# A gated attention and feed-forward block on one core: the mask as one row, fp16 row maxima, constant products in TensorE's early waits, and the range check's squares moved to turns 3 to 6

## The reference

```
logits = einsum('bhqd,bhkd->bhqk', Q * 32**-0.5, K) + b        # Q from layernorm(x), 8 heads of 32
weights = softmax(logits - 1e30 * (1 - mask))                  # mask is 1 only where a key counts
x = x + tanh(g_xattn) * einsum('bhqk,bhkd->bhqd', weights, V)
gate, up = einsum('bsd,hd->bsh', layernorm(x), wg), einsum('bsd,hd->bsh', layernorm(x), wu)   # w / 127, 768 hidden
x = x + tanh(g_ffn) * einsum('bsh,dh->bsd', silu(gate) * up, wd)
```

## Time and profile before

| | us |
|---|---|
| median of 3 runs | 160.29 (159.06 to 160.47) |
| the profiled execution | 158.84 |
| its span in the trace | 157.0 |
| busy: PE, VectorE, ScalarE, GpSimd | 132.8, 122.4, 92.9, 90.9 |

### The profile page before, as it was taken

One profiled execution on the slowest core, in us unless ns is written; L12 is line 12 of the kernel. 1 busy time (PEld: TensorE's weight loads), 2 busy tenths in 40 slices (PEclk: granted clock), 3 DMA queues, 4 the chain that ended last, 5 costly groups with the idle time before them and its releaser, 6 DMA issues.

```text
span 157.0 us, 4000 instructions
## 1 busy us (share of the span) xinstructions
PE 132.8 (85%) x1363; PEld 99.9 (64%) x1363; DVE 122.4 (78%) x348; ACT 92.9 (59%) x203; POOL 90.9 (58%) x139
## 2 busy tenths in 40 slices
PE   0656789957898997999899999998999998899970
PEld 0233557735477685858695878678777777676750
DVE  3799899999998988997899699567924937766631
ACT  4327789967556483738373748553877654465530
POOL 6254450542755794689465956645674678774530
PEclk9999999999999999999999999999999999999997
DMA  4499910000006002921171216250100020020022
GB/s 134 134 364 373 363 44 0 6 0 0 4 0 134 6 19 48 136 71 34 33 138 67 40 33 134 71 69 0 43 28 0 0 71 0 0 69 4 0 73 75
DMA packets 19928, 11.06 MB, mean 70 GB/s; under 512 B 13488, under 2 KB 19136, under 8 KB 19904
## 3 DMA queue, kind: packets, MB, share of 16 engines
q1 hardware_dynamic: 19728, 10.49, 25.6%
q10 hardware_dynamic: 176, 0.27, 0.5%
HBM read 5.51 MB, written 2.10 MB: 48 GB/s over the span
## 4 chain that ended last, share of the span: by engine, by line
PE 34%; DVE 27%; POOL 12%; DMA 11%; issue 10%; ACT 3%; SPq 1%; POOLq 0%; DVEq 0%; ACTq 0%
PE ps L1339 13%; DMA n_t<-norm 8%; PE ps L1361 6%; DVE neg_max L1019 4%; DVE stats L911 4%; DVE gated L1068 3%; DMA gates<-in_L_xattn_b_dram 3%; POOL norm L675 3%; POOL rstd L646 3%; POOL norm L668 2%; PE ps L1274 2%; PE ps L1268 2%; DVE x_sb L890 2%; PE ps L1288 2%; DVE h L1079 2%
## 5 line engine op out<-in xcount | busy, mean ns | idle before, releaser
L1339 PE MATMUL ps<-n_t,w_gu_t 128*128 128x256 f16 x384 | 49.9, 273 | 3.3 <-DMA n_t<-norm 2.2
L1339 PEld LDWEIGHTS ps<-n_t,w_gu_t 128*128 128x128 f16 x384 | 36.2, 98 | 13.1 <-DMA n_t<-norm 4.2
L692 POOL TENSOR_TENSOR h<-h 128x256 f16<-128x256 f32 x48 | 32.2, 673 | 15.0 <-ACT h L832 14.8
L823 ACT ACTIVATE tanh_h<-ps 128x256 f32<-128x256 f32 x48 | 18.3, 382 | 21.0 <-PE ps L1339 20.8
L1361 PE MATMUL ps<-w_d_t,h 128*128 128x256 f16 x192 | 28.3, 272 | 0.8 <-DVE x_sb L890 0.4
L1019 DVE TENSOR_REDUCE neg_max<-ps 128x4 f32<-128x512 f32 x32 | 21.5, 685 | 6.5 <-PE ps L1218 6.5
L1068 DVE SCALAR_TENSOR_TENSOR gated<-tanh_h,ps 128x256 f32<-128x256 f32 x48 | 19.7, 411 | 6.1 <-ACT tanh_h L823 6.1
L646 POOL TENSOR_TENSOR rstd<-var_eps,neg_half 128x2 f32<-128x2 f32 x16 | 11.1, 696 | 21.4 <-DVE var_eps L918 21.3
L776 ACT ACTIVATE probs<-ps,key_bias 128x512 f32<-128x512 f32 x32 | 21.9, 684 | 2.5 <-PE ps L1247 2.4
L832 ACT ACTIVATE h<-h 128x256 f16<-128x256 f32 x48 | 19.8, 412 | 5.7 <-DVE h L1079 5.2
L1079 DVE SCALAR_TENSOR_TENSOR h<-ps,gated 128x256 f32<-128x256 f32 x48 | 20.3, 424 | 1.7
...
## 6 DMA issues: line engine op xcount, KB each, us to landing
...
q_stacks<-q_parts SPq DMA_TRANSPOSE x8, 3.2
```

The source lines that it names most:

```text
L692: pool.tensor_tensor(h16[:, r % 2, m, 1, :], h32[:, n % NHB, :], h16[:, r % 2, m, 0, :], ALU.subtract).then_inc(h_low, 1)
L823: act.activation(tanh_h[:, n % 2, :], bank32(HID_BANKS[n % 2])[:, 0:SH], ACT.Tanh, scale=0.5 * W_SCALE).then_inc(tanh_done, 1)
L1339: ins = pe.matmul(dst, lhs, rhs, start=(w == 0 and (k, l) == terms[0]), stop=(k, l) == terms[-1], skip_group_check=True)
```

## The change

- **Mask.** A DMA loads the last 128 mask values of all batches into one partition (`mask_row`), and one VectorE operation makes `bias_row` of it (0 or -42496). The row maxima add this row by a matmul with one row of ones. The exponentials take `exp_bias`, four columns, two small operations. `mask_t` stays for the check and for `exp_bias`; the split of the bias, its four transposes and their copy are left to the wide path.
- **Maxima.** The reduction writes its fp16 result straight into what `max_t` transposes; `max_split` is gone from the narrow path in all eight blocks. The selector is fp16 too, and the key limit of the check is 7500.
- **Loads.** The first keys are loaded by SP's queue behind the first rows; the gates behind the second keys. The low part of the first keys moves from GpSimd to VectorE (`k_rest`).
- **Constant products.** 30 matmuls on constants in six places of the front (8, 2, 4, 4, 9, 3) in place of 8 in one, into the bank of the feed-forward's result.
- **Squares and check.** The ten squares leave the front and turns 0 and 1 and stand at places 1, 3 and 5 of turns 3, 4 and 5 and place 1 of turn 6; `check` and `flag_sum` at places 2 and 3 of turn 6.

The diff, cut to its core:

```diff
-WARM_UP = 8
-K_LIMIT = 60000.0
+WARM_UP = (8, 2, 4, 4, 9, 3)
+K_LIMIT = 7500.0
+SHUT_OUT = -42496.0
...
-    steps = [("stats", 1, 0), ("mask_t",), ("warm_up",), ("norm1", 0), ("high", 1, 0), ("low", 1, 0), ("k_parts", 0),
-             ("mask_parts",), ("mask_rows",), ("dup", 0), ("stats", 1, 1), ("q_stack", 0, 0), ("k_stack", 0),
-             ("norm1", 1), ("q_stack", 0, 1), ("high", 1, 1), ("low", 1, 1), *maxima(0)[:3], ("dup", 1),
-             *maxima(0)[3:], sq(0), ("q_stack", 0, 2), ("max_split", 0), ("max_t", 0), ("q_stack", 0, 3),
-             ("k_parts", 1), ("stats", 1, 2)]
-
-    chores = [[sq(1)], [("w_cast", 0)], [sq(2), sq(3)], [("k_stack", 1)], [("w_t", 0), sq(4)],
-              [("w_cast", 1), ("w_t", 1), sq(5)],
-              [sq(6), sq(9)], [("w_t", 2)], [sq(7), ("w_t", 3)], [sq(8), ("check",)], [("flag_sum",), ("y_scale",)], [("w_cast", 2)],
-              [("w_t", 4)], [("w_t", 5)], [], [("k_parts", 2)], [("k_stack", 2)]]
+    steps = [("bias_row",), ("stats", 1, 0), ("warm_up", 0), ("k_parts", 0), ("norm1", 0), ("k_rest", 0),
+             ("high", 1, 0), ("low", 1, 0), ("mask_cast",), ("dup", 0), ("warm_up", 1), ("k_stack", 0),
+             ("stats", 1, 1), ("warm_up", 2), ("q_stack", 0, 0), ("q_stack", 0, 1), ("mask_t",), ("norm1", 1),
+             ("high", 1, 1), ("low", 1, 1), ("warm_up", 3), *maxima(0)[:2], ("exp_bias",), maxima(0)[2], ("dup", 1),
+             *maxima(0)[3:], ("warm_up", 4), ("q_stack", 0, 2), ("max_t", 0), ("q_stack", 0, 3), ("k_parts", 1),
+             ("stats", 1, 2), ("warm_up", 5)]
+
+    chores = [[], [("w_cast", 0)], [], [("k_stack", 1)], [("w_t", 0)], [("w_cast", 1), ("w_t", 1)],
+              [], [("w_t", 2)], [("w_t", 3)], [], [("y_scale",)], [("w_cast", 2)],
+              [("w_t", 4)], [("w_t", 5)], [], [("k_parts", 2)], [("k_stack", 2)], []]
+    chores += [part for i in range(10) for part in ([], [sq(i)])] + [[("check",)], [("flag_sum",)]]
...
-        put(("max_split", r + 1), when=ahead)
...
             load_x(sp, 0)
+            load_kv(sp, 0)
+            load_x(sp, 1)
+            load_kv(sp, 1)
             for n, g in enumerate((g_xattn, g_ffn, attn_b)):
                 sp.dma_start(gates[:, n:n + 1], g.partition_broadcast(P)).then_inc(gates_loaded, 16)
-            load_x(sp, 1)
-            load_kv(sp, 1)
...
-                    elif kind == "k_parts":
+                    elif kind == "k_parts" and step[1]:
...
+            act.dma_start(mask_row[:, :, :], mask[:, LAST * P:SK].unsqueeze(0)).then_inc(mask_row_loaded, 16)
             act.dma_start(mask_raw[:, :], mask.rearrange("b (c k) -> (b c) k", k=P)).then_inc(mask_loaded, 16)
-            load_kv(act, 0)
             act.wait_ge(pool_done, CONSTS)
-            act.activation(max_sel[:, :, :], head_rows[:, :].unsqueeze(2).to_broadcast((P, NH, P)), ACT.Copy
...
-                                       bias=key_bias[:, n:n + 1]).then_inc(exp_done, 1)
+                                       bias=key_bias[:, n:n + 1] if is_wide else exp_bias[:, b:b + 1]
+                                       ).then_inc(exp_done, 1)
...
-                dve.wait_ge(mask_loaded, 16)
-                dve.tensor_copy(mask_f[:, :], mask_raw[:, :]).then_inc(mask_cast, 1)
                 dve.wait_ge(work_filled, plan.filled(step))
                 dve.tensor_copy(mask_k[:, :], bank32(plan.bank(step))[:, 0:B * NC]).then_inc(emptied_by["dve"], 1)
                 dve.wait_ge(*plan.emptied(step))
+                mine(dve.tensor_scalar(exp_bias[:, :], last_mask, -1.0, 1.0, ALU.mult, ALU.add))
+                mine(dve.tensor_scalar(checks[:, 0:B * NC], mask_k[:, :], 0.0, None, ALU.not_equal))
+                mine(dve.tensor_scalar(checks[:, NZERO:NZERO + B], last_mask, 1.0, None, ALU.is_ge))
+                wait_mine()
+
+                mine(dve.scalar_tensor_tensor(
+                    out=checks[:, 0:B * NC].rearrange("p (b c) -> p b c", c=NC)[:, :, LAST], in0=last_mask, scalar=0.0,
+                    in1=last_mask, op0=ALU.not_equal, op1=ALU.not_equal))
+
+            def exp_bias_steps():
+
+                dve.wait_ge(gates_loaded, 48)
+                mine(dve.tensor_scalar(exp_bias[:, :], exp_bias[:, :], MASK_STEP, gates[:, 2:3], ALU.mult, ALU.add))
+                wait_mine()
+
+                dve.tensor_scalar(exp_bias[:, :], exp_bias[:, :], gates[:, 2:3], 0.0, ALU.subtract, ALU.min
+                                  ).then_inc(exp_bias_ready, 1)
+
+            def mask_parts_steps():
...
+                    elif kind == "bias_row":
+
+                        dve.wait_ge(mask_row_loaded, 16)
+                        dve.tensor_scalar(bias_row[:, :, :], mask_row[:, :, :], -SHUT_OUT, SHUT_OUT, ALU.mult, ALU.add
+                                          ).then_inc(bias_row_ready, 1)
+                    elif kind == "mask_cast":
+                        dve.wait_ge(mask_loaded, 16)
+                        dve.tensor_copy(mask_f[:, :], mask_raw[:, :]).then_inc(mask_cast, 1)
                     elif kind == "mask_t":
                         mask_steps(step)
+                    elif kind == "exp_bias":
+                        exp_bias_steps()
...
+                    elif kind == "k_rest":
+
+                        b = step[1]
+                        dve.wait_ge(k_high, b + 1)
+                        full, high, low = key_parts(b)
+                        dve.tensor_tensor(low, full, high, ALU.subtract).then_inc(k_low, 1)
...
+                        h, first = 2 * b + qt // 2, qt % 2 == 0 and g == 0
                         if is_wide:
+                            n = plan.nth[WIDE + "max_split", h]
+                            if first and n >= 2:
+                                dve.wait_ge(max_split, n - 1)
                             dst = max_c[:, qt, g * HG:(g + 1) * HG, c]
                         else:
-                            dst = neg_max[:, qt, g * HG:(g + 1) * HG]
+                            if first and h == 0:
+                                dve.wait_ge(zeros_written, 1)
+                            if first and h >= 2:
+                                dve.wait_ge(work_filled, plan.filled(("max_t", h - 2)))
+
+                            dst = max_cols16[:, qt, g * HG:(g + 1) * HG]
...
-                        for _ in range(WARM_UP):
-                            pe.matmul(bank32(SCORES[0]), ones_b[:, :], ones_b[:, :].unsqueeze(1).to_broadcast((P, HG, P)),
+                        for _ in range(WARM_UP[step[1]]):
+                            pe.matmul(bank32(Y_BANK), ones_b[:, :], ones_b[:, :].unsqueeze(1).to_broadcast((P, HG, P)),
...
-                        rows = bias_rows[:, b * NC + c, :].unsqueeze(1).to_broadcast((P, HG, P))
-                        pe.matmul(bank32(n), ones_b[:, :], rows, start=False, stop=True, skip_group_check=True
+                        if is_wide:
+                            ones, rows = ones_b[:, :], bias_rows[:, b * NC + c, :].unsqueeze(1).to_broadcast((P, HG, P))
+                        else:
+                            pe.wait_ge(bias_row_ready, 1)
+                            ones, rows = ones_b[0:1, :], bias_row[:, b, :].unsqueeze(1).to_broadcast((1, HG, P))
+                        pe.matmul(bank32(n), ones, rows, start=False, stop=True, skip_group_check=True
...
+                        h = step[1]
+                        if is_wide:
+                            pe.wait_ge(max_split, plan.nth[WIDE + "max_split", h] + 1)
+                        else:
+                            pe.wait_ge(*plan.emptied(("row_max", h // 2, LAST, 2 * (h % 2) + 1, NG - 1)))
...
-                            ins = pe.matmul(dst, max_sel[:, h, :], max_rows[:, rows, :], start=False, stop=True,
+                            ins = pe.matmul(dst, (max_sel if is_wide else max_sel16)[:, h, :],
+                                            (max_rows if is_wide else max_rows16)[:, rows, :], start=False, stop=True,
```

More of the change, by code:

```diff
@@ L379, in flamingo_block_kernel @@
         recip = sb("recip", [P, 2, NH], F32)
+        mask_row = sb("mask_row", [1, B, P], I32)
+        bias_row = sb("bias_row", [1, B, P], BF16)
+        exp_bias = sb("exp_bias", [P, B], F32)
+        max_cols16 = sb("max_cols16", [P, QT, P], F16)
+        max_rows16 = max_rows[:, :, :].rearrange("p n s -> p (n s)").bitcast(F16).rearrange("p (n s) -> p n s", n=2)
+        last_mask = mask_k[:, :].rearrange("p (b c) -> p b c", c=NC)[:, :, LAST]
+        max_sel16 = kv_rest[:, 0, :].bitcast(F16).rearrange("p (h k) -> p h k", h=NH)
         max_parts = max_cols[:, :, 0:NPART * NH].rearrange("p t (a h) -> p t a h", a=NPART)
@@ L1026, in run @@
                         dve.wait_ge(*plan.emptied((row_max, b, LAST, 2 * (h % 2) + 1, NG - 1)))
-                        if n >= 2:
-                            before = plan.of_kind["max_t"][n - 2]
-                            dve.wait_ge(work_filled, plan.filled(before))
-                        if n == 0:
-                            dve.wait_ge(zeros_written, 1)
```

(8 more changed lines are left out.)

51 lines of the change are left out of this document (26 added, 25 removed).

## The result

| | before | after |
|---|---|---|
| median of 20 runs each, us | 160.09 (158.87 to 161.87) | 158.89 (158.41 to 159.92) |
| profiled execution, us | 158.84 | 158.58 |
| its span, us | 157.0 | 156.5 |

The ratio of after to before is 0.9956, 95% interval 0.9935 to 0.9977. That is 0.7 us of 160, where 2.8 were forecast. Both kernels' runs spread over more than 1 us, before's in two groups, near 159 and near 160.3, and its profiled execution is of the lower one. So the two medians lie 1.2 us apart and the two profiled executions 0.26. Medians, ranges and ratios of the experiments are of the runs within 1.5% of the kernel's fastest; four of seven lay outside in experiment 2 (165.06 to 167.09 us) and three of twelve in experiment 7 (159.26 to 160.23).

A forecast was written before the change was run, and what follows sets the result against it. Bound by a chain alternating TensorE and VectorE; in turns 3 and 4 a 15.4 us loop through the DMA. 0.3 + 0.5 + 2.0 = 2.8 us off 158.84 gives 156.0, plus 1.45 for the median: 157.5 us, range 155.0 to 160.0.

The forecast's parts named there:

- front: Work ahead of the first scores: `dup` 1 starts earlier unless `exp_bias` is held beside GpSimd; 0.3 us (-0.2 to 1.0).
- turn 0: VectorE loses a split of 0.72 us, so the queries' copy comes forward; gain 0.5 us (0.2 to 0.72).
- turn 1: VectorE loses split, comparison and `flag_sum`, TensorE its 1.76 us wait; gain 2.0 us (1.7 to 2.3).
- turns 2 to 5: Loop through TensorE, VectorE, GpSimd, ScalarE, DMA: removed splits only lengthen VectorE's wait; 0, at most 0.89 + 0.66 us.
- its matmul with one row: Bias row added to the row maxima by one row instead of 128, same 512 columns: costed at nothing.
- Squares: Ten squares moved into ScalarE's free time in turns 3 to 6: 0 cost, at most 6.6 us.
- The check: Check and flag moved to turn 6, the comparison not late there: 0 cost, at most 1.76 us.
- B: VectorE, free earlier each turn, lets TensorE's waits of 0.89 and 0.66 us vanish: 155.9 us, chance 0.17.
- C: TensorE's clock at 1.2 GHz for the first transposes, front up to 1.0 us behind: 158.8 us, chance 0.11.
- E: The check's wait covered another in turns 0 and 1; only some 1 us comes through: 159.3 us, chance 0.14.
- D: Squares delay tanhs or exponentials and lengthen the loop, up to 6.6 us: 164.1 us, chance 0.06.
- The base: Median of the runs lies 1.45 us above the profiled execution's 158.84, so 156.0 becomes 157.5 us.

The follow-up runs named there:

- experiment 2: The kernel before, with the matmul that adds the mask's bias taking 3 rows instead of 128: 162.61 us, ratio 1.0181.
- experiment 7: The changed kernel with 128 rows in the bias product and 8 constant products at one place instead of 30 at six: 158.28 us, ratio 0.9889.
- experiment 1: The changed kernel with 128 rows (127 of them zero) in the bias product instead of one: 156.26 us, ratio 0.9784.
- experiment 9: The changed kernel with 96 rows (95 of them zero) in the bias product: 156.31 us, ratio 0.978.
- experiment 10: The changed kernel with 64 rows (63 of them zero) in the bias product: 159.11 us, ratio 0.9971.
- experiment 6: The changed kernel with 128 bias rows, check and flag later, and `exp_bias` behind all maxima of block 0: 155.33 us, ratio 0.9706.
- experiment 8: The changed kernel with 128 bias rows, and squares, check and flag at the places of the kernel before: 156.74 us, ratio 0.9794.
- experiment 4: The changed kernel with squares, check and flag at the places of the kernel before: 158.97 us, ratio 0.9953.
- experiment 3: The kernel before with only squares, check and flag moved to where the change puts them: 160.03 us, ratio 0.9999.

## Why the prediction was wrong

The steps of the profiled executions, forecast against measured (the last column with the row's cost taken away, experiment 1):

| step | forecast | after | 128 rows |
|---|---|---|---|
| front, to the first exponential | 0.3 | 0.36 | 0.51 |
| turn 0 | 0.5 | 0.30 | 0.85 |
| turn 1 | 2.0 | 1.25 | 1.95 |
| turns 2 to 5 | 0 | -0.8 | 0.0 |
| turn 6 | 0 | -0.65 | -0.2 |
| sum | 2.8 | 0.45 | 3.1 |

**The step that failed** is the one costed at nothing: "its matmul with one row (same 512 columns)". Columns did not change, and the product is as long as before; but with one row the weight loads on both sides of it no longer run ahead, 0.2 us each time, 32 times. Experiments 1, 2, 9 and 10 show it from both kernels: 2.7 us at the end of the profile, 2.8 between the medians with 96 and 64 rows. The prediction looked at the duration of the product and not at the distance between starts, and at VectorE's savings only; for an engine that the windows showed 14.98 us busy of 15.8 in turn 4, anything added was to be priced.

**The front** went as priced: `exp_bias` was held until GpSimd ended (0.81 us; 0.22 where nothing runs beside it, experiment 6), `dup` 1 at 15.24 in the range 15.1 to 15.5. The statistics and the low part came 0.8 us earlier, where 0.7 to 1.0 was forecast (VectorE's work between 8.74 and 10.23 is 1.49 us, not 1.4), and the held operation used it up.

**Turn 0** gave 0.85 without the row's cost, more than the 0.72 of the split. The squares, given no gain of their own, do not hold the rest: experiment 8, with the squares at their old places, also gave 0.85 (-0.46 to -1.31). What does stays open.

**Turn 1** was sized right: 1.95 with 128 rows, of which the moved work is 1.4 (experiment 8 against 1) and the split some 0.5. The eight one-row products of turns 0 and 1 took 0.55 us of turn 0 and 0.70 of turn 1.

**The loop of turns 2 to 5** held as argued, with 128 rows: the starts stay behind the DMA, 15.4 and 15.6 us apart, and VectorE's and ScalarE's savings there are worth nothing. With one row, four products a turn add 0.8 us to TensorE, which ate the waits of 0.89 and 0.66 us and then, in turn 5, the gain. The forecast used these waits as an upper bound on gains; they were a cushion for losses. The fourth unit is an exception: with 128 rows it starts 14.4 us behind the third (14.9 in before) and without before's wait of 0.49, which gives 0.57 us in experiments 1 and 8. The forecast's bound had left this wait out.

**Squares** at nothing: right (no product waited for a tanh behind one). **The check** in turn 6 at nothing: wrong by 0.8 us. The comparison was not late, as argued; the cost is `flag_sum`'s product, for which VectorE waits 0.62 us, and its four small operations, 0.98 us, ahead of the attention's reciprocal. The forecast counted TensorE's wait and left out what stood behind the flag on VectorE. Placed later it cost 0.3.

**The rivals.** B, the loop giving way: the opposite came, for a reason not among the rivals. C, a low clock in the front: not in the profiled execution, where the transposes at 7.65 ran at the upper level; in experiment 4's, with the same products ahead, they did not, and 0.5 us were lost. Experiment 7 shows how large the term can be: with 8 products in the new order 1.7 us are lost. E: turn 1's wait covered nothing (with 128 rows turn 2 began 3.2 us early), though in after turn 2 began only 1.85 us early, between the 2.5 to 3 of the forecast and the 1 of E; read by that sign alone the cause would have been mistaken. D: no.

**The base.** The forecast added 1.45 us, the distance of before's median from its profiled execution. After's is 0.3 (158.89 and 158.58). Its profiled time was forecast at 156.0 and is 158.58, 2.5 us more; the smaller distance took 1.1 of that back, and the median forecast (157.5) missed by 1.4: a smaller miss by chance and not by a right term. (The bounds of the terms add up to 1.7 to 4.0, not 1.5 to 4.0; nothing hangs on it.) Two traces suggest what before's two groups of runs are: in before's, 158.84 us, the transposes of the front ran at the upper level, in experiment 3's, 160.26, at the lower, 0.96 us later. One trace of each doesn't show it. Experiments 1 and 7 suggest that the constant products narrow the spread (0.4 us with 30, 2.3 with 8), but after's own runs still spread over 1.5.
